# Attention with the maxima split on GpSimd, copied on ScalarE, and the second pass masked by GpSimd selects

## The reference, cut to what matters

```python
scores = jnp.einsum('bhqd,bhkd->bhqk', q, k) * scale     # 16 heads of 8 columns, 512 tokens
causal = jnp.tril(jnp.ones((t, t), bool))
scores = jnp.where(causal, scores, -jnp.inf)
attn = jax.nn.softmax(scores, axis=-1)
out = jnp.einsum('bhqk,bhkd->bhqd', attn, v)
...
x = x + gt_a[:, None, :] * (out @ Wproj + bproj)
xn = _layernorm(x, g2, be2)
...
x = x + gt_m[:, None, :] * (h @ W2 + b2)
```

## Time and profile before

| | us |
|---|---|
| median of 3 runs (lowest, highest) | 270.11 (270.01, 271.88) |
| the profiled execution, as timed | 272.03 |
| its span in the profile | 270.2 |
| TensorE busy, of the span | 163.4 |
| VectorE busy | 190.4 |
| ScalarE busy | 144.2 |
| GpSimd busy | 77.4 |

### The profile page before, as it was taken

One profiled execution on the slowest core, in us unless ns is written; L12 is line 12 of the kernel. 1 busy time (PEld: TensorE's weight loads), 2 busy tenths in 40 slices (PEclk: granted clock), 3 DMA queues, 4 the chain that ended last, 5 costly groups with the idle time before them and its releaser, 6 DMA issues.

```text
span 270.2 us, 4240 instructions
## 1 busy us (share of the span) xinstructions
PE 163.4 (60%) x1515; PEld 101.4 (38%) x1519; DVE 190.4 (70%) x530; ACT 144.2 (53%) x315; POOL 77.4 (29%) x90
## 2 busy tenths in 40 slices
PE   0222137907632400630846967898998998796985
PEld 0102034606521300300833524645545545453654
DVE  0688787899996798497588578759778878614411
ACT  3455769277796403594414542536545645775431
POOL 6243612235306334297015972000000000003110
PEclk9999999965575555595779977579999999999999
DMA  5995000000000000000000450321000000000011
GB/s 141 417 428 235 1 0 0 0 0 4 0 0 1 0 0 0 0 1 0 2 0 32 101 95 11 60 46 20 5 2 4 2 4 2 2 5 0 2 39 39
DMA packets 4491, 11.50 MB, mean 43 GB/s; under 512 B 1267, under 2 KB 2644, under 8 KB 3828
## 3 DMA queue, kind: packets, MB, share of 16 engines
q1 hardware_dynamic: 3510, 10.04, 11.1%
q0 software_dynamic: 960, 1.19, 2.1%
HBM read 8.24 MB, written 0.52 MB: 32 GB/s over the span
## 4 chain that ended last, share of the span: by engine, by line
DVE 40%; PE 37%; POOL 6%; ACT 5%; issue 5%; DMA 4%; SPq 1%; DVEq 0%
DVE negmax L1172 8%; PE ps L1522 6%; PE ps L1327 5%; PE ps L1462 4%; POOL uh L444 4%; PE ps L1552 3%; PE ps L1558 3%; DMA cw<-in_cond_w 2%; PE ps L1502 2%; DVE xhat L833 2%; DVE u L990 2%; PE ps L1409 2%; DVE mx L1073 2%; DVE bnst L820 2%; DMA QS<-nmT 1%
## 5 line engine op out<-in xcount | busy, mean ns | idle before, releaser
L1172 DVE TENSOR_REDUCE negmax<-ps 128x1 f32<-128x384 f32 (+3 forms) x96 | 52.9, 595 | 17.8 <-PE ps L1464 17.7
L730 ACT ACTIVATE PT<-ps 128x1024 f32<-128x1024 f32 x40 | 40.7, 1025 | 36.7 <-PE ps L1508 36.3
L377 POOL TENSOR_TENSOR rstd<-veps,mhalf 128x4 f32<-128x4 f32 x8 | 8.3, 1034 | 116.5 <-DVE veps L827 116.5
L1462 PE MATMUL ps<-KS,QS 48*128 48x384 bf16 (+3 forms) x128 | 33.9, 333 | 1.1 <-DVE negmax L1172 0.8
L1327 PE MATMUL ps<-k_f,u 128*128 128x128 f32 x40 | 10.0, 425 | 33.2 <-ACT u L642 23.4
L1502 PE MATMUL ps<-QS,KS 51*128 51x512 bf16 (+3 forms) x128 | 24.9, 319 | 0.9 <-DMA QS<-nmT 0.9
L1463 PE MATMUL ps<-k_b 64*128 64x128 bf16 x128 | 25.1, 234 | 0.0
L1522 PE MATMUL ps<-PT,V 128*9 128x512 f32 (+3 forms) x256 | 23.3, 448 | 1.9 <-ACT PT L730 1.2
L1464 PE MATMUL ps<-k_b 64*128 64x64 bf16 x128 | 22.2, 199 | 0.0
L1327 PEld LDWEIGHTS ps<-k_f,u 128*128 128x128 f32 x40 | 7.6, 220 | 35.2 <-DVE u L990 27.8
L1462 PEld LDWEIGHTS ps<-KS,QS 48*128 48x128 bf16 x128 | 11.1, 97 | 20.3 <-DVE negmax L1172 14.2
(11 more groups left out here) (207 smaller groups left out, 457.8 us busy)
## 6 DMA issues: line engine op xcount, KB each, us to landing
w<-in_wa SPq DMA_DIRECT2D x2, 1152.0 KB, 10.8
lw<-in_l_w SPq DMA_DIRECT2D x1, 1280.0 KB
brow<-in_bcast_rows SPq DMA_DIRECT2D x1, 1152.0 KB, 15.6
mw<-in_main_w SPq DMA_DIRECT2D x1, 1024.0 KB, 13.6
KS<-part POOLq DMA_DIRECT2D x12, 64.0 KB, 3.9
QS<-part SPq DMA_DIRECT2D x12, 64.0 KB
cw<-in_cond_w SPq DMA_DIRECT2D x1, 576.0 KB, 6.0
xs<-in_x SPq DMA_DIRECT2D x1, 512.0 KB, 7.6
```

What stands on the lines that cost most here:

```text
L377: return nc.gpsimd.tensor_tensor(r, v, mhalf[0:v.shape[0], 0:v.shape[-1]], ALU.pow)
L730: nc.scalar.activation(PT[n % 2][:, s, :], bank(2 * (use % 2), 2), ACT.Exp).then_inc(S["p_ready"], 1)
L1172: V.tensor_reduce(negmax[n % 2][:, qt, h0:h0 + nh], bank(S_BANKS[k % 3])[:, 0:nh * w].rearrange("p (h w) -> p h w", w=w), AX.X, ALU.max, n ...
L1462: T.matmul(dst, QS[b][rows, h, tok(qt)], KS[b][rows, h, 0:w], start=True, stop=False)
```

## The change

Four things are changed together.

1. The split of the maxima moves from VectorE to GpSimd, as four instructions with a semaphore between each two (`split_maxima`). VectorE's reduction of item 0 waits for the split of the group before last, whose buffer it writes.
2. The copy of the transposed maxima moves from VectorE to ScalarE, between the exponentials of slots 3 and 4, and has its own semaphore `nm_copied`; `bank_free` now says which of the two semaphores a bank's reuse waits for.
3. The causal mask of the second pass is no longer added by products. The exponentials run over all columns (`p_exp`), and GpSimd sets the future ones of each diagonal block to 0 in PT by `affine_select` (`drop_future`), which now counts `p_ready`. A bank of a slot is free after the exponential. The mask constants of the keys are dropped.
4. The value products of a group are made in two bursts, kt = 0 and 1 at i = 5, kt = 3 and 2 at i = 9, and the transposes of the group before (`values_rows`) move from i = 3 to i = 2, ahead of score 3.

GpSimd's two roots and adds at the end become `norm_root(b)`; the first stands in round 8 behind the select of slot 2, and ahead of the selects of slots 3 and 4 of the last group; the second at the end.

```diff
@@ constants
-PV_AT = {5: 0, 6: 1, 7: 3, 10: 2}
+PV_AT = {5: (0, 1), 9: (3, 2)}
@@ SyncE
             for n in range(B * NG):
-                sp.wait_ge(S["s_used"], NUMBER[n, "maxima"] + 1)
+                sp.wait_ge(S["nm_copied"], n + 1)
@@ GpSimd
-            for b in range(B):
+            def split_maxima(n):
...
+                pool.wait_ge(S["s_used"], len(S_ITEMS) * (n + 1))
+                nc.gpsimd.tensor_copy(pt[:, :, :, 0, :], nm).then_inc(S["nm_hi"], 1)
+                pool.wait_ge(S["nm_hi"], n + 1)
+                nc.gpsimd.tensor_tensor(left, nm, pt[:, :, :, 0, :], ALU.subtract).then_inc(S["nm_left"], 1)
+                pool.wait_ge(S["nm_left"], n + 1)
+                nc.gpsimd.tensor_copy(pt[:, :, :, 1, :], left).then_inc(S["nm_mid"], 1)
+                pool.wait_ge(S["nm_mid"], n + 1)
+                nc.gpsimd.tensor_tensor(pt[:, :, :, 2, :], left, pt[:, :, :, 1, :], ALU.subtract
+                                        ).then_inc(S["nm_ready"], 1)
+            def drop_future(n, s):
+                diagonals = [(0, 2, L)] if s < 2 else [(0, 2, L), (3 * P, 2, L)] if s < 4 else [(0, 4, 2 * P)]
+                pool.wait_ge(S["p_exp"], 5 * n + s + 1)
+                for at, count, step in diagonals:
+                    v = PT[n % 2][:, s, :].rearrange("p (c w) -> p c w", w=step)[:, :, at:at + P]
+                    ins = nc.gpsimd.affine_select(v, v, [[0, count], [1, P]], ALU.is_ge, 0.0, base=0,
+                                                  channel_multiplier=-1)
+                ins.then_inc(S["p_ready"], 1)
+            def norm_root(b):
                 pool.wait_ge(S["ln_var"], 3 * B + b + 1)
                 root(rstd[:, tiles(b)], veps[:, tiles(b)]).then_inc(S["ln_root"], 1)
                 pool.wait_ge(S["xhat_ready"], B + b + 1)
                 nc.gpsimd.tensor_tensor(xs[:, tiles(b), :], xs[:, tiles(b), :], over_tiles(b2_g[:, b, :]), ALU.add
                                         ).then_inc(S["biased"], 1)
+            for n in range(N_GROUPS + 2):
+                if n >= 2:
+                    for s in (3, 4):
+                        drop_future(n - 2, s)
+                if 1 <= n <= N_GROUPS:
+                    for s in (0, 1):
+                        drop_future(n - 1, s)
+                if n < N_GROUPS:
+                    split_maxima(n)
+                if 1 <= n <= N_GROUPS:
+                    drop_future(n - 1, 2)
+                if n == N_GROUPS:
+                    norm_root(0)
+            norm_root(1)
@@ ScalarE, exp_slot and the loop
-                                     ).then_inc(S["p_ready"], 1)
+                                     ).then_inc(S["p_exp"], 1)
+            def copy_maxima(n):
+                k = NUMBER[n, "maxima"]
+                act.wait_ge(S["s_pe"], k + 1)
...
+                nc.scalar.activation(nmT[n % 2][:, :], bank(S_BANKS[k % 3])[0:3 * HG, 0:L // 2].bitcast(BF16), ACT.Copy
+                                     ).then_inc(S["nm_copied"], 1)
-                for lag, slots in ((2, (3, 4)), (1, (0, 1, 2))):
...
+                if 2 <= n <= N_GROUPS + 1:
+                    exp_slot(n - 2, 3)
+                if 1 <= n <= N_GROUPS:
+                    copy_maxima(n - 1)
+                if 2 <= n <= N_GROUPS + 1:
+                    exp_slot(n - 2, 4)
+                if 1 <= n <= N_GROUPS:
+                    for s in range(3):
+                        exp_slot(n - 1, s)
...
@@ VectorE: row_maxima, and split_maxima and copy_maxima leave it
+                if n >= 2 and i == 0:
+                    dve.wait_ge(S["nm_ready"], n - 1)
@@ TensorE
+            def bank_free(k):
+                if k >= 3 and USES[k - 3][1] == "maxima":
+                    pe.wait_ge(S["nm_copied"], USES[k - 3][0] + 1)
+                elif k >= 3:
+                    pe.wait_ge(S["s_used"], SCORES[k - 3])
@@ exp_slot
                 if use >= 2:
-                    pe.wait_ge(S["p_ready"], use - 1)
+                    pe.wait_ge(S["p_exp"], use - 1)
...
-                        T.matmul(dsts[half], KS[b][rows, h, tok(kt)], QS[b][rows, h, kt * P:L], start=True, stop=False)
-                    for half in range(2):
-                        r = half_rows(2 * half)
-                        T.matmul(dsts[half][:, 0:P // 2], k_of("pickLo", r), k_of("maskKlo", r), start=False, stop=False)
-                    for half in range(2):
-                        r = half_rows(2 * half)
-                        ins = T.matmul(dsts[half][:, 0:P], k_of("pickHi", r), k_of("maskKhi", r), start=False, stop=True)
+                        ins = T.matmul(dsts[half], KS[b][rows, h, tok(kt)], QS[b][rows, h, kt * P:L],
+                                       start=True, stop=True)
@@ the loop
+                    if i == 2 and n >= 3:
+                        values_rows(n - 3)
...
-                    if i == 3 and n >= 3:
-                        values_rows(n - 3)
                     if i in PV_AT and 2 <= n <= N_GROUPS + 1:
-                        values(n - 2, PV_AT[i])
+                        for kt in PV_AT[i]:
+                            values(n - 2, kt)
```

More of the change, by code:

```diff
@@ L67 @@
 KC, KC_N = _spans(("ident", P), ("pickLo", P), ("pickHi", P), ("maskQlo", P), ("maskQhi", P // 2),
-                  ("maskKlo", P // 2), ("maskKhi", P), ("count", 16), ("kone", 1))
+                  ("count", 16), ("kone", 1))
 W4_ROUND = (0, 1, 2, 5)
@@ L106, in _rotation @@
                 order.append((n - 1, "maxima"))
-    return {what: k for k, what in enumerate(order)}
-NUMBER = _rotation()
+    return order
+USES = _rotation()
+NUMBER = {what: k for k, what in enumerate(USES)}
+SCORES = [sum(i != "maxima" for _, i in USES[:k + 1]) for k in range(len(USES))]
 S_BANKS = (4, 5, 7)
@@ L463, in _ @@
                                         ).then_inc(S["biased"], 1)
-            for b in range(B):
+            def split_maxima(n):
+                nm = negmax[n % 2][:, :, :].rearrange("p t (a h) -> p t a h", a=2)
+                left = nmrest[:, :, :].rearrange("p t (a h) -> p t a h", a=2)
+                pt = nmpart[n % 2]
+                pool.wait_ge(S["s_used"], len(S_ITEMS) * (n + 1))
[16 more added lines that the diff above has]
+            def norm_root(b):
                 pool.wait_ge(S["ln_var"], 3 * B + b + 1)
@@ L738, in _ @@
                     nc.scalar.activation(pvs[(n - 3) % 2][:, :], bank(6), ACT.Copy).then_inc(S["pv_ready"], 1)
-                for lag, slots in ((2, (3, 4)), (1, (0, 1, 2))):
-                    if 0 <= n - lag < N_GROUPS:
-                        for s in slots:
-                            exp_slot(n - lag, s)
-                            if n == N_GROUPS and s == 0:
-                                columns_of_attention(0)
+                if 2 <= n <= N_GROUPS + 1:
[7 more added lines that the diff above has]
+                        exp_slot(n - 1, s)
+                        if n == N_GROUPS and s == 0:
+                            columns_of_attention(0)
             modulate_columns(0, 1)
@@ L1174, in row_maxima @@
                                 AX.X, ALU.max, negate=True).then_inc(S["s_used"], 1)
-            def split_maxima(n):
-                nm = negmax[n % 2][:, :, :].rearrange("p t (a h) -> p t a h", a=2)
-                left = nmrest[:, :, :].rearrange("p t (a h) -> p t a h", a=2)
-                pt = nmpart[n % 2]
-                dve.wait_ge(S["s_used"], NUMBER[n, len(S_ITEMS) - 1] + 1)
-                then(V.tensor_copy(pt[:, :, :, 0, :], nm))
-                then(V.tensor_tensor(left, nm, pt[:, :, :, 0, :], ALU.subtract))
-                then(V.tensor_copy(pt[:, :, :, 1, :], left))
-                V.tensor_tensor(pt[:, :, :, 2, :], left, pt[:, :, :, 1, :], ALU.subtract
-                                ).then_inc(S["nm_ready"], 1)
-            def copy_maxima(n):
-                k = NUMBER[n, "maxima"]
-                dve.wait_ge(S["s_pe"], k + 1)
-                if n >= 2:
-                    dve.wait_ge(nm_stacked[n % 2], 32 * (n // 2))
-                V.tensor_copy(nmT[n % 2][:, :], bank(S_BANKS[k % 3])[0:3 * HG, 0:L // 2].bitcast(BF16)
-                              ).then_inc(S["s_used"], 1)
             def divide(n):
@@ L1221, in _ @@
                         split_last(1)
-                    if i == 2 and 1 <= n <= N_GROUPS:
-                        copy_maxima(n - 1)
                     if i == 3 and n >= 3:
@@ L1578, in _ @@
                         exp_slot(n - 1, E_NEW[i])
-                    if i == 3 and n >= 3:
-                        values_rows(n - 3)
                     if i in PV_AT and 2 <= n <= N_GROUPS + 1:
-                        values(n - 2, PV_AT[i])
+                        for kt in PV_AT[i]:
+                            values(n - 2, kt)
                     if n == N_GROUPS and i == 7:
-                        pe.wait_ge(S["s_used"], NUMBER[N_GROUPS - 1, "maxima"] + 1)
+                        pe.wait_ge(S["nm_copied"], N_GROUPS)
```

(1 more changed line is left out.)

17 lines of the change are left out of this document (8 added, 9 removed).

## The result

| | kernel before | changed kernel |
|---|---|---|
| median of its runs | 270.06 us (269.3 to 271.88) | 280.81 us (278.37 to 285.21) |
| ratio | | 1.038, 95% interval 1.034 to 1.042 |
| profiled execution | 272.03 us, span 270.2 | 278.37 us, span 276.5 |
| matmuls | 1515 | 1259 |

An execution over 1.5% above the fastest of its kernel (here 285.21 us) is left out of the ratio, but not of the median. The sign and the range held; the time lies 4.1 us above the forecast. The profiled execution of the changed kernel is the fastest of its four, and that of the kernel before lies 1.9 us above its median. So the spans of the two traces differ by 6.3 us and the medians by 10.7. The four executions of the changed kernel order themselves by TensorE's mean granted clock: 278.37 us at 0.827, 279.39 at 0.809, 282.23 at 0.799, 285.21 at 0.795. The kernel before stays between 0.840 and 0.854.

What follows compares the result with a forecast made beforehand. No engine binds alone; TensorE and VectorE alternate in the attention rounds. Ramp -0.9, rounds +1.1, last transfer +0.4, tail queue +3.7 and clock +2.3 sum to +6.6, so 276.7 us, range 271.5 to 281.5.

Steps and rivals of the forecast that it cites:

- tail queue: Last group: selects of slots 3 and 4 wait behind GpSimd's bias add for batch 0, delaying the last value products; +3.7 us.
- T to M: Each round, from the end of the four last reductions to the maxima's transposes, with the split on GpSimd: 1.2 us.
- Rival (c): GpSimd is dear on the split: T to M 2.2 us, period 10.96, total 282.7 us; chance 0.12.
- (b): GpSimd is cheap: T to M 0.65 us, period 9.41, tail +1.9, total 269.3 us; chance 0.15.
- M to the value product: Each round, from the maxima's transposes to the first value product, which waits for VectorE's quotient: 2.80 us, before 2.42.
- The period: One attention round at full clock: 9.96 us, 0.22 longer than before, +1.1 us over five periods.
- Selects: GpSimd's masking of exponentials: 0.73 us over 256 columns, 1.27 over 512, 5.7 us a group, hidden in the rounds.
- rival d: The first select has a start-up cost, delaying the second group's split in the ramp; upper end 280 us; chance 0.06.
- The ramp: First rounds at half clock: fewer mask products and shorter slots give -0.9 us, between 0 and -2.
- The last transfer: Last group, from the last reductions to exponent slot 0: 4.96 us instead of 4.55, with the copy on ScalarE; +0.4.
- The gap on TensorE: Sign that the forecast is right: TensorE idle over 3 us at the last group's selects, half clock behind it.
- Clock: TensorE falls to half clock behind its wait for selects in the tail: +2.3 us, between 0 and 4.5.

Runs made afterwards that it cites:

- div_first: The changed kernel, but VectorE divides ahead of the reduction of score 3 instead of behind it; 278.54 us, ratio 1.034 to the kernel before.
- t_add: The changed kernel, but GpSimd's bias add for batch 0 stands behind the last group's selects of slots 3 and 4; 278.27 us, ratio 1.023 to the kernel before.
- fill_only: The changed kernel with its 256 mask products of the second pass put back on TensorE beside the selects; 276.93 us, ratio 1.026 to the kernel before.
- no_sel: The changed kernel without its selects, the mask products of the second pass kept on TensorE; 272.4 us, ratio 1.009 to the kernel before.
- both: The changed kernel with the bias add behind the last group's selects and VectorE dividing ahead of score 3's reduction; 275.33 us, ratio 1.022 to the kernel before.
- both_fill: The kernel `both` with the 256 mask products put back on TensorE beside the selects; 268.32 us, ratio 0.995 to the kernel before.

## Why the prediction was right, and where it fell short

- **The side and the range** held, and so did the likeliest case: the tail queue and a period that grows. But 276.7 us was 4.1 short. Over the two profiled spans the sum looks met, +6.6 forecast and +6.3 measured, and that is luck: errors of either sign cancel, as the terms below show.
- **T to M**: 1.2 forecast, 1.27 measured. The value of 0.22 for a 128x16 operation, from the line through the two products in the earlier trace rows, was met exactly (0.20 for the casts). Rival (c), dear GpSimd, falls; the low end of (b), 0.65, too.
- **M to the value product**: 2.80 forecast, 2.84 measured, with VectorE's division behind score 3 as its cause, which div_first shows (M to value product 1.9, period 9.03).
- **The period**: 9.96 forecast, 9.99 measured; five times 0.25 for five times 0.22.
- **Selects**: forecast at 0.73 and 1.27, measured 0.41 and 0.635. The line through both gives 0.9 ns a column and 0.18 fixed: the memset's rate in the earlier trace rows, not the compare's. Of the two rows I took the wrong neighbour. The Trainium skill ("GPSIMD Engine Reference", section "Engine selection") says that one-input work runs roughly at line rate on GpSimd. The selects agree with it: VectorE's reductions of 384 and 512 columns, 0.55 and 0.68 us on the mean, are 1.0 ns a column apart. The compare at 2.86 ns a column doesn't. So the tail queue cost 2.4 us instead of 3.7. The forecast's "2.5 with cheap selects" was itself a slip: its selects of 0.23 and 0.46 give 1.8, about what rival (b) has. The gap on TensorE that it named as a sign, over 3 us, was 2.17.
- **No start-up cost (rival d)**: the first select took 0.42 us, like all others, and began at 169.86, some 0.07 us behind the end of its exponential (168.77, and half of the 2.04 us that two of them take). The Trainium skill ("GPSIMD Engine Reference", section "Instruction dispatch") puts the first call of freshly loaded code near 6 us, without a visible instruction in the profile. Neither the record of this select nor the time ahead of it holds such a cost.
- **The ramp**: -0.9 forecast, -1.75 measured, but for other reasons. 0.9 was there at the first score (152.10 against 153.00), and some 0.8 more came in the scores of the first group, where the clock stood at 1.00 between 158 and 163 us and at 0.66 in the trace of before. Neither is the change's as far as the traces tell. Behind the first transposes of maxima, where the forecast looked for its 0.9, only 0.16 was won.
- **The last transfer**: +0.4 forecast. It was covered: slot 0 waited for the value products at half clock.
- **The step that failed** is the one headed *Clock*. It looked for the clock's fall in the one long wait of the tail only, +2.3, where 1.3 was measured; and even there the clock fell at 247.2, ahead of that wait, and it fell in t_add without it. It costed the masks' removal at "0.64 us a group" of TensorE time that is idle anyway, and had no term for what that idle time does to the clock in the rounds. In the profiled execution there were two falls of 1.5 us in the late rounds, of which putting the products back removes the first; over the runs it is 3.9 us at the median (changed kernel against fill_only). The spread of the runs goes with their mean clock. The sentence that "what TensorE saves ahead of it on masks is idle" named the condition, and stopped there. The Trainium skill ("TensorE: Matmul & The Clock Gate", section "A second HAM failure mode: psum-queue depth-cycling") describes such a case in another kernel: short idles between groups of matmuls are enough for the clock to swing between its two levels. This trace agrees, with idles of 0.28, 0.65 and 0.89 us a round and no longer wait until the clock falls at 226. But no_sel, with 0.65 and 0.72, kept its clock in the rounds, so the idles alone do not tell when it falls. It would have been a term, or a rival of its own.

What stays open is which property of the 256 products holds the clock up, since the runs put all of them back or none; why the fall comes in one round and not in its twin before it; and what brings the one behind the last maxima, which comes with and without the products.

## What to carry to other kernels

Taking cheap products off TensorE, in a loop in which it is already idle for other reasons, can lose: here the saved time was no gain and the clock went with it. Price the idle time that an edit leaves behind as well as the work it removes, and ask of every edit that lightens TensorE whether its full clock is still fed. On an in-order queue, look for the late instruction that a new one is placed behind: here one bias add ahead of the selects of two slots cost 2.4 us, and moving it removed that.

## What the runs showed of the hardware that was not expected

- 256 matmuls that change nothing in the result made a kernel 7.0 us faster (275.33 to 268.32), and another 3.9 us (280.81 to 276.93), and the granted clock went back from 0.84 to 1.00 in the rounds (both against both_fill) and from 0.83 to 1.00 from 222 to 232 us (changed kernel against fill_only).
- The granted clock fell to half at 226.7 us of the changed kernel behind idle times of TensorE of at most 0.90 us, and at 247.2 while products were running.
- Sixteen value products of 512 and 384 columns take 1.69 us at full clock and 3.15 at half; their instructions scale with the clock nearly whole.
- An affine select on GpSimd in place took 0.41 us for 128x256 and 0.635 for 128x512 in f32, a small cast 0.20, and a dependent small operation follows its predecessor's start by 0.28 us. On VectorE the same four follow by 0.21.
- With the products in place, 14.8 us of GpSimd work in 40 us of rounds left the period the same as 3.1 us did (10.08).
